# Low-rank second factors copied inside SBUF instead of through DRAM: two adapter layers in float32 parts

## The reference, cut to what matters

```
# x: (8, 128, 512), float32; one W0 of eight and one LoRA pair per batch
c0  = einsum('bsi,boi->bso', x, weight[itok_B_3_7])                 # layer 0, per-batch W0
y   = einsum('bsd,od->bso', c0, W1) + bias                          # layer 0, W1 shared
low = einsum('bsr,bor->bso', einsum('bsd,brd->bsr', c0, A0), B0)    # rank 16, adapter by segment
x1  = x + y + where(use_lora, low, 0)
c1  = x1 @ W2.T + b2 + scale * (x1 @ a1.T) @ b1.T                   # layer 1, rank 16 per batch
out = x1 + (c1 @ W3.T + b3) + routed experts of rank 32 on c1       # needs a max over all tokens
```

## Time and profile before

| | |
|---|---|
| Median of 3 runs | 135.06 us (134.25 to 137.37) |
| The profiled execution, its own time | 134.48 us |
| Its span, first to last instruction | 132.5 us |
| PE busy / weight loads | 120.9 us (91%) / 103.3 us (78%) |
| DVE / ACT / POOL busy | 83.6 us (63%) / 56.5 us (43%) / 22.5 us (17%) |
| Mean granted TensorE clock | 0.974 |
| DMA | 23.04 MB, 174 GB/s over the span |

### The profile page before, as it was taken

How to read it: one execution, slowest core, us unless ns; L and a number is a source line. 1 busy time by engine, 2 the same in 40 slices (tenths; PEclk the granted TensorE clock), 3 DMA queues, 4 the chain that set the end, 5 groups by cost and what they waited for, 6 DMA issues and landing times.

```text
span 132.5 us, 1890 instructions
## 1 busy us (share of the span) xinstructions
PE 120.9 (91%) x703; PEld 103.3 (78%) x703; DVE 83.6 (63%) x172; ACT 56.5 (43%) x94; POOL 22.5 (17%) x30
## 2 busy tenths in 40 slices
PE   6999999999829999999818999999989999999992
PEld 2488777888719999998717898999978878688891
DVE  0599299848967496754299376087995557431671
ACT  3374499459977374905914613153051011031000
POOL 3077815040047505000041000000000000000000
PEclk9999999999995999999997799999999999999999
DMA  3999965999389993896980000000000000000673
GB/s 108 383 393 413 404 251 140 332 398 327 95 357 380 294 329 101 287 376 203 409 326 4 0 0 0 5 0 0 0 0 0 5 0 0 0 0 0 227 272 137
DMA packets 7752, 23.04 MB, mean 174 GB/s; under 512 B 800, under 2 KB 1184, under 8 KB 7488
## 3 DMA queue, kind: packets, MB, share of 16 engines
q1 hardware_dynamic: 4784, 13.06, 26.7%
q0 software_dynamic: 2624, 9.44, 20.3%
q10 hardware_dynamic: 336, 0.44, 0.9%
HBM read 18.64 MB, written 4.29 MB: 173 GB/s over the span
## 4 chain that ended last, share of the span: by engine, by line
PE 59%; DMA 15%; DVE 15%; issue 4%; ACT 3%; SPq 1%; ACTq 0%; DVEq 0%
PE bank L851 45%; DMA b_rows<-c_lo 7%; DVE w_lo L542 5%; DMA x_in<-in_x 5%; DMA b<-b_rows 4%; PE bank L963 3%; PE bank L953 3%; DVE c_row L747 2%; PE bank L956 2%; PE bank L959 2%; DVE m_lo L581 2%; PE bank L888 1%; DVE bm_parts L740 1%; DVE x_lo L533 1%; ACT w_hi L381 1%
## 5 line engine op out<-in xcount | busy, mean ns | idle before, releaser
L336 POOL DMA_INDIRECT w_in<-in_W,rows_i x16 | 16.8, 1048 | 30.4 <-DVE w_lo L542 12.5
L851 PE MATMUL bank<-c_hi,w_hi 128*128 128x256 f32 x64 | 18.8, 294 | 2.9 <-DMA b<-b_rows 2.9
L542 DVE TENSOR_TENSOR w_lo<-w_in,w_hi 128x1024 fp32r<-128x1024 f32 x16 | 19.1, 1220 | 2.8 <-ACT w_hi L381 2.7
L851 PE MATMUL bank<-c_lo,w_hi 128*128 128x256 f32 x64 | 18.8, 294 | 0.0
L851 PE MATMUL bank<-c_hi,w_lo 128*128 128x256 f32 x64 | 18.8, 294 | 0.0
L381 ACT CAST w_hi<-w_in 128x1024 fp32r<-128x1024 f32 x16 | 16.1, 1047 | 3.5 <-DMA w_in<-in_W,rows_i 3.5
L851 PE MATMUL bank<-w_hi,x_hi 128*128 128x512 f32 x32 | 13.7, 428 | 3.1 <-issue 2.9
L851 PEld LDWEIGHTS bank<-c_hi,w_hi 128*128 128x128 f32 x64 | 12.8, 200 | 3.2 <-issue 3.0
L851 PE MATMUL bank<-m_hi,x_hi 128*128 128x512 f32 (+1 forms) x36 | 13.8, 385 | 0.0
L851 PE MATMUL bank<-m_hi,x_lo 128*128 128x512 f32 (+1 forms) x36 | 13.2, 367 | 0.0
L851 PE MATMUL bank<-w_hi,x_lo 128*128 128x512 f32 x32 | 13.2, 413 | 0.0
(11 more groups left out here) (181 smaller groups left out, 241.9 us busy)
## 6 DMA issues: line engine op xcount, KB each, us to landing
w_in<-in_W SPq DMA_DIRECT2D x5, 512.0 KB, 4.9
x_in<-in_x SPq DMA_DIRECT2D x4, 512.0 KB, 7.3
out_dram<-w_in SPq DMA_DIRECT2D x7, 256.0 KB, 3.0
be<-be_rows SPq DMA_DIRECT2D x1, 1120.0 KB, 5.1
b<-b_rows SPq DMA_DIRECT2D x1, 1024.0 KB, 4.7
w_in<-in_W SPq DMA_DIRECT2D x1, 1024.0 KB, 9.1
be_rows<-low_t SPq DMA_DIRECT2D x1, 840.0 KB, 5.2
b_rows<-c_lo SPq DMA_DIRECT2D x1, 768.0 KB, 4.6
```

The costliest lines, as they stand in the source:

```text
L336: nc.gpsimd.indirect_dma_start(w_in[:, slot, half * h:half * (h + 1)], None, W0, row).then_inc(w_landed[b][h], 16)
L542: nc.vector.tensor_tensor(part(w_lo[:, b % 2], h), raw(b, h), f32(part(w_hi[:, b % 2], h)), ALU.subtract).then_inc(w_lo_done, 1)
L851: ins = mm(o, st, mv, start=start and n == 0, stop=stop and n == len(parts) - 1)
```

## The change

1. The trip through DRAM is gone. `spread` now issues, for each pair i and each of the 4 groups g, one SBUF to SBUF copy of 32 rows: 16 transfers of 64 KB for `b0` and 16 of 70 KB for `be`, all on SP. The rows of the adapter tables are ordered by batch, so that a pair's 32 rows lie together, and the transposes of the first factors lose their reordering view (`by_pair`).
2. SP's list: W1 waits for the first half of W0 of batch 1 instead of for g0. Then b0 of pairs 0 and 1, x of pair 2 (no longer behind W0 of batch 3), b0 of pairs 2 and 3, x of pair 3, and the 16 copies of `be`.
3. PE waits for `b0_landed[i]` of its pair only; `low1_high(0)` on ACT waits for all 16 copies of `be` instead of the stores; DVE waits for all copies of `b0` before `c0_low(2)`.
4. Order of the lists: the split of `b0` goes ahead of `w_high(1)`/`w_low(1)`; the last split of `be` goes from behind `x1_high(0, 1)` to ahead of `w_high(3)`/`w_low(3)`; the split of `bm` goes from the tail into the loop's last round, ahead of `x1_high(2, 1)`/`x1_low(2, 1)`.

```diff
@@ SP
-            sp.wait_ge(g0_landed, 16)
             sp.wait_ge(w2_lo_done, 4)
             sp.wait_ge(w3_lo_done, 4)
+            sp.wait_ge(w_landed[1][0], 16)
             ...
-            def spread(parts, rows, stored):
-                src = f32(parts[:, 0]).unsqueeze(1).to_broadcast([P, G - 1, parts.shape[-1]])
-                sp.dma_start(rows[0:G - 1].rearrange("g p d -> p g d"), src).then_inc(stored, 16)
-                sp.dma_start(rows[G - 1], f32(parts[:, 1])).then_inc(stored, 16)
-            def gathered(rows):
-                return rows.rearrange("g (k i) d -> (g k) (i d)", i=NP)
+            def spread(t, parts, i, landed):
+                for g in range(G):
+                    sp.dma_start(f32(t[K2 * g:K2 * (g + 1), i]),
+                                 f32(parts[K2 * i:K2 * (i + 1), 0 if g < G - 1 else 1])).then_inc(landed, 16)
             sp.wait_ge(b0_hi_done, 1)
             sp.wait_ge(b0_done, 1)
-            spread(b0_parts, b0_rows, b0_stored)
-            sp.wait_ge(b0_stored, 32)
-            sp.dma_start(f32(flat(b0[:])), gathered(b0_rows)).then_inc(b0_landed, 16)
+            spread(b0, b0_parts, 0, b0_landed[0])
+            spread(b0, b0_parts, 1, b0_landed[1])
             sp.wait_ge(a0_ready, 1)
-            sp.wait_ge(w_landed[3][1], 16)
             load_x(2)
+            spread(b0, b0_parts, 2, b0_landed[2])
+            spread(b0, b0_parts, 3, b0_landed[3])
+            sp.wait_ge(a1_ready, 1)
+            load_x(3)
             ...
-            spread(be_parts, be_rows, be_stored)
-            sp.wait_ge(a1_ready, 1)
-            load_x(3)
-            sp.wait_ge(be_stored, 32)
-            sp.dma_start(f32(flat(be[:])), gathered(be_rows)).then_inc(be_landed, 16)
+            for i in range(NP):
+                spread(be, be_parts, i, be_landed)
@@ low1_high
-                    act.wait_ge(be_stored, 32)
+                    act.wait_ge(be_landed, 16 * NP * G)
@@ ACT
             nc.scalar.copy(flat(b1_hi), bank[7][:]).then_inc(b1_hi_done, 1)
+            act.wait_ge(g0_landed, 16)
+            nc.scalar.copy(b0_parts[:, 0], rows0[:, D:2 * D]).then_inc(b0_hi_done, 1)
             ...
             w_high(1)
-            act.wait_ge(g0_landed, 16)
-            nc.scalar.copy(b0_parts[:, 0], rows0[:, D:2 * D]).then_inc(b0_hi_done, 1)
@@ ACT (DVE's list changes in the same places, with the lo parts)
             low0_high(0)
+            act.wait_ge(bes_summed, 1)
+            nc.scalar.copy(be_parts[:, 0, D:], bes_f[:]).then_inc(bes_hi_done, 1)
             w_high(3)
             ...
+                if i == NP - 1:
+                    act.wait_ge(late_landed, 16)
+                    nc.scalar.copy(bm_parts[:], bm4).then_inc(bm_hi_done, 1)
                 x1_high(i - 1, 1)
@@ DVE
             x_low(2)
+            for i in range(NP):
+                dve.wait_ge(b0_landed[i], 16 * G)
             c0_low(2)
@@ layer_b
-                    pe.wait_ge(b0_landed, 16)
+                if h == 0:
+                    pe.wait_ge(b0_landed[i], 16 * G)
```

More of the change, by code:

```diff
@@ L52, in place, with build @@
         at += w
-def build(nc, x, W0, W1, W23, g0, g1, scale, early, al, late, b0_rows, be_rows, out):
+def build(nc, x, W0, W1, W23, g0, g1, scale, early, al, late, out):
     ctx = ExitStack()
@@ L167, in build @@
         g0_landed, g1_landed, s_landed = sem("g0_landed"), sem("g1_landed"), sem("s_landed")
-        b0_stored, be_stored, w3_landed = sem("b0_stored"), sem("be_stored"), sem("w3_landed")
-        b0_landed, be_landed = sem("b0_landed"), sem("be_landed")
+        w3_landed = sem("w3_landed")
+        b0_landed, be_landed = [sem(f"b0_landed{i}") for i in range(NP)], sem("be_landed")
         late_landed = sem("late_landed")
@@ L490, in _ @@
             nc.scalar.copy(ae[:, :, 0:NS], ae_f[:]).then_inc(ae_hi_done, 1)
-            act.wait_ge(bes_summed, 1)
-            nc.scalar.copy(be_parts[:, 0, D:], bes_f[:]).then_inc(bes_hi_done, 1)
             for i in range(2, NP):
@@ L504, in _ @@
                 c0_high(2 * i + 1)
+                if i == NP - 1:
+                    act.wait_ge(late_landed, 16)
+                    nc.scalar.copy(bm_parts[:], bm4).then_inc(bm_hi_done, 1)
                 x1_high(i - 1, 1)
-            act.wait_ge(late_landed, 16)
-            nc.scalar.copy(bm_parts[:], bm4).then_inc(bm_hi_done, 1)
             low0_high(NP - 1)
@@ L614, in bits @@
                                                  ALU.logical_shift_right, ALU.bitwise_and))
-                bits(1, 0, NP - 1)
-                bits(2, 2, RANK - 1)
-                bits(3, 6, 1)
+                bits(1, 5, NP - 1)
+                bits(2, 0, RANK - 1)
+                bits(3, 4, 1)
                 bits(4, 4, 1)
@@ L670, in _ @@
             nc.vector.tensor_tensor(flat(b1_lo), bank[7][:], f32(flat(b1_hi)), ALU.subtract).then_inc(b1_lo_done, 1)
-            w_low(1)
             dve.wait_ge(b0_hi_done, 1)
@@ L674, in _ @@
                                     ALU.subtract).then_inc(b0_done, 1)
+            w_low(1)
             dve.wait_ge(aet_ready, 1)
@@ L701, in _ @@
             low0_low(0)
+            dve.wait_ge(bes_hi_done, 1)
+            nc.vector.tensor_tensor(be_parts[:, 1, D:], bes_f[:], f32(be_parts[:, 0, D:]),
+                                    ALU.subtract).then_inc(bes_done, 1)
             w_low(3)
@@ L714, in _ @@
             nc.vector.tensor_tensor(ae[:, :, NS:2 * NS], ae_f[:], f32(ae[:, :, 0:NS]), ALU.subtract).then_inc(ae_done, 1)
-            dve.wait_ge(bes_hi_done, 1)
-            nc.vector.tensor_tensor(be_parts[:, 1, D:], bes_f[:], f32(be_parts[:, 0, D:]),
-                                    ALU.subtract).then_inc(bes_done, 1)
             for i in range(2, NP):
@@ L730, in _ @@
                 c0_low(2 * i + 1)
+                if i == NP - 1:
+                    dve.wait_ge(bm_hi_done, 1)
+                    for a in (1, 3):
+                        at = slice(R * a, R * (a + 1))
+                        nc.vector.tensor_tensor(bm_parts[at], bm4[at], f32(bm_parts[at]),
+                                                ALU.subtract).then_inc(bm_done, 1)
                 x1_low(i - 1, 1)
@@ L736, in _ @@
             low1_low(NP - 2)
[L737 to L740, removed]
             dve.wait_ge(w3_landed, 16)
@@ L939, in layer_low1, with turn_rows @@
                 low_rank(bank[7][:, 0:2 * S], a1, i, x_hi[:, i], x_lo[:, i]).then_inc(low1_ready, 1)
-            def turn_rows(o, rows, by_pair):
+            def turn_rows(o, rows):
                 for c in range(C):
                     to = chunk(o[:], c)
-                    last = nc.tensor.transpose(to.rearrange("p (i k) -> p k i", k=K2) if by_pair else to, chunk(rows, c),
+                    last = nc.tensor.transpose(to, chunk(rows, c),
                                                ident[:])
@@ L981, in _ @@
             pe.wait_ge(ident_done, 1)
-            turn_rows(bank[7], rows1[:, D:2 * D], False).then_inc(b1_ready, 1)
+            turn_rows(bank[7], rows1[:, D:2 * D]).then_inc(b1_ready, 1)
             layer_a(0)
@@ L997, in _ @@
             pe.wait_ge(g0_landed, 16)
-            turn_rows(bank[6], rows0[:, 0:D], True).then_inc(a0_ready, 1)
+            turn_rows(bank[6], rows0[:, 0:D]).then_inc(a0_ready, 1)
             layer_a(1)
@@ L1011, in _ @@
                             [(small_parts[:, c], b2_parts[:, c]) for c in range(C)]).then_inc(smalls_ready, 1)
-                    turn_rows(bank[5], rows1[:, 0:D], True).then_inc(a1_ready, 1)
+                    turn_rows(bank[5], rows1[:, 0:D]).then_inc(a1_ready, 1)
                 layer_low0(i - 1)
@@ L1056, in _ @@
             pe.wait_ge(ae_done, 1)
-            pe.wait_ge(be_landed, 16)
+            pe.wait_ge(be_landed, 16 * NP * G)
             pe.wait_ge(c0_saved, NB)
@@ L1161 @@
     g0 = np.concatenate([np.zeros((RANK, 2 * D), np.float32), table(v["L0_ffn_lora_A"], v["L0_ffn_lora_B"])])
-    by_rank = np.broadcast_to(v["itok_B_1_7"].reshape(NP, 2).T[:, None, :], (2, RANK, NP))
+    by_rank = np.repeat(v["itok_B_1_7"], RANK)
     ids = np.concatenate([np.broadcast_to(v["itok_B_3_7"], (P, NB)), by_rank.reshape(P, 1),
@@ L1182 @@
         args.append(nc.dram_tensor("in_" + name, a.shape, mybir.dt.from_np(a.dtype), kind="ExternalInput").ap())
-    args.append(nc.dram_tensor("b0_rows", (G, K1, D), F32, kind="Internal").ap())
-    args.append(nc.dram_tensor("be_rows", (G, K1, D + NS), F32, kind="Internal").ap())
     args.append(nc.dram_tensor("out_dram", (NB, S, D), F32, kind="ExternalOutput").ap())
```

## The result

The changed kernel takes 128.9 us (median of 4 runs, 128.15 to 129.42) against 136.04 us before (4 runs, 134.25 to 137.37): a ratio of 0.957, 95% interval 0.946 to 0.967. It is faster by 4.3%, where 125.2 us had been forecast. The profiled execution took 129.24 us (span 126.9) against 134.48 (132.5): 5.2 us less, not 9.1.

What follows compares the result with a forecast made beforehand. PE, busy 91%, was taken to lose time in two big stops and the slow clock behind each. Removing them, less 1.0 us in the middle, plus 0.1 for bm, gave 9.1 us: 125.4, stated as 125.2, range 123.3 to 129.3 (about 85%).

Steps and rivals of the forecast that it cites:

- both stops: Before layer_b(0, 0) (`b`) and layer_a(6) (late `be`): gains 3.4 and 3.5 us, plus 1.5 and 1.6 of slow clock.
- bm account: `bm` split leaves DVE's tail: new 0.6 us stop at low1(2), one of 0.6 removed; gain 0.0 to 0.1.
- the sum: 3.4 + 1.5 + 3.5 + 1.6 - 1.0 + 0.1 = 9.1 us off the profiled 134.48, hence 125.4.
- The start: layer_b(0, 0) starts at 36.6 in place of 40.02 us: gain 3.4, bounds 2.9 to 5.1.
- the term of 1.0 us for the middle: Short new PE stops, 0.5 us at turn_c0(3), 0.3 at low0_low(1) and their like: 1.0 given back, bounds 0 to 3.
- the bad end: `be` up to 4 us late at 0.7 us per copy; ACT stops 52 to 56, giving back perhaps 3 us.
- Rival (c): W0 of batch 4 lands 2 us later; PE stops 2 to 3 us at turn_c0(3) or layer_a(4): 127 to 129, 14%.
- (b): `be` partly late, 0.6 to 0.8 us per copy; 2 to 4 us stop before layer_a(6) remains: 128 to 131, 12%.
- The third mis-sized step: Before layer_b(0, 0): early W1 brings W0 of batch 2 some 2 us earlier, W1's lo part 0.6 us earlier.
- layer_a(6) near 61.5: Sign of being right: layer_a(6), behind the second big stop at 69.92 us before, starts near 61.5 us.
- 134.25 - 10.7: Whole kernel, if all stops go and the middle gives nothing back: 123.5 us.
- The rule that spoke against it: Many small transfers should be one; some 2 us each, sixteen copies in a row 35 us if they did not overlap.

Runs made afterwards that it cites:

- the edit alone: The kernel with `be` as two held-back DRAM writes and `b0` by 16 copies, with the split of bm back in the tail: 124.91 us, ratio 0.927.
- fast version: Changed kernel, but `be` goes through DRAM, its 2 writes held until both halves of W0 of batch 4 landed; `b0` keeps 16 copies: 124.87 us, ratio 0.929.
- second profiled execution of the changed kernel: The changed kernel run again with no edit, beside three other kernels: 129.55 us, ratio 0.962, span 126.4.
- fourth experiment: Kernel before, still through DRAM, with the rest of the change (early W1, early x of pairs 2 and 3, splits moved): 130.44 us, ratio 0.984.
- quiet stretch: 68 to 82 us of the fast version, where one run added unused transfers inside SBUF with nothing else in flight: 124.15 us, span 122.2.

## Why the prediction missed

**What held.** The reading of both stops was right, and so was their removal in kind: no wait for `b`, x_high(3) without a wait, the clock at full from 20 to 90 us in both profiled executions (1.5 us given back twice: from layer_b(0, 0), 2.0 us early, to turn_c0(2), 3.4 us early, and from layer_a(6), 4.1 us early, to the end, 5.6 us early). W1 was issued at 16.98 as worked out. The bm account (one stop of 0.6 in, one out) was shown by the edit alone. The fast version's profiled execution has a span of 123.3 us and 125.0 us of time, against 125.4 of the sum, but that is in part luck: its start is 0.9 us later than forecast (37.53), and it gives nothing back in the middle, where 1.0 had been forecast.

**Where the 3.5 us are.** The sum made the span 132.5 - 9.1 = 123.4 us; it was 126.9. Three terms account for it. The start brought 1.97 us, not 3.4: 1.4 short. The middle gave back 2.24 + 0.59 = 2.8 us, not 1.0: 1.8 short. The last 0.2 lie behind layer_a(6). (The time outside the span grew by another 0.3 us, from 2.0 to 2.3.) In the second profiled execution of the changed kernel the start was as forecast (36.71, 3.3 us) and the middle gave back 1.53 + 2.15 = 3.7.

**The step that failed** is the term of 1.0 us for the middle, with `be` in time at no cost, and it rests on the price of a copy: "16 copies at SP's 0.39 us end their issue at 44.6 ... I let them land by 48". The 0.39 us came from a write to DRAM, the nearest row. A copy inside SBUF holds SP's queue for 0.62 us alone and 0.68 us in place; `be` was ready for its first copy at 39.78 (1.5 us later than worked out), the last copy was issued by 50.6, and ScalarE had them at 57.44, 6.8 us after that, where 3.4 had been allowed. So `be` was 9.4 us late: 1.5 by its start, 4.5 by the issues, 3.4 by the landing. That cost PE 0.59 us in one execution and 2.15 in the other. The prediction had named 0.7 us as the bad end ("a landing of `be` after 52 us"), and gave that case only 12%. The rows offered nothing inside SBUF, so the range of this price should have had the same weight at both ends, and 16 of them in series on one path multiply it.

**The other part of that term** is the gather of W0 of batch 4. Rival (c) had the right place and too small a chance: the gather took 7.9 and 7.2 us instead of 6.1, the stop at turn_c0(3) was 2.24 and 1.53 us instead of 0.5. By what `be` had in flight beside it, the gather took:

| `be` beside the gather | us, one execution each |
|---|---|
| 16 copies inside SBUF | 7.9, 7.2, 7.3, 6.2 |
| trip through DRAM, hi written three times | 8.2 |
| two writes to DRAM | 6.8 |
| nothing, held back until it had landed | 5.5, 5.2, 6.3, 5.9, 5.6, 5.3 |
| nothing, old order, x of pair 2 just ahead | 6.5 |

Holding `be` back removed the stop, for the copies (2.24 and 1.53 to nothing) as for the two writes (1.1 to nothing). So it is contention with `be` in flight, and the trip's 8.2 us speak against a special price of the copies: `be` goes out 14 us earlier than before, by either route. The rows overlap (6.2 with the 16 copies, 6.3 and 6.5 without), so the size of it is not settled by these single executions; the 8.2 is one execution too. That the early `be` does both things was not in the prediction: it had (b) and (c) as separate cases, and they came together.

**The third mis-sized step** is the start: "W0 of batch 2 comes 2 us earlier or so" when W1 is out of the way. Its halves came 0.1 and 0.9 us later in the profiled execution, and W1's lo part, issued 3.2 us earlier, ended 0.9 later; the 1.97 us gained lie below the bound of 2.9 "with no gain from W1". In the other profiles of this kind the first half was cast between 25.7 and 27.7. Across the profiles with the early W1 and the 16 copies of `b0` the start lies between 36.3 and 38.1. The copies beside that gather may be the cause; no run shows it, and with only 4 of them the start was 36.84, inside that spread.

**Two slips in the arithmetic.** "layer_a(6) near 61.5" leaves out the 1.0 us which the sum gives back in the middle: it should be 62.5, and 65.79 is 1.4 (start) and 1.8 (middle) behind that. PE's own work between layer_b(0, 0) and layer_a(6) was right: 24.9 us net of stops, as before (69.92 - 40.02 - 0.6 - 2.9 - 1.5). And the lower bound "134.25 - 10.7" does not follow from the terms, which give 10.1 without the middle, so 124.2.

**The rule that spoke against it.** The Trainium skill ("DMA: Bandwidth & Descriptors", Rules for kernel authors) wants many small transfers made one. As advice it was right: two writes in the place of sixteen copies, held back until the gather had landed, took 4.6 us off the kernel (129.55 against 124.91 us in one group, the latter also with the bm split in the tail, which is worth nothing). The writes alone, not held back, gave 126.73 us in another group, some 2 to 3 us less than the changed kernel's 128.9 and 129.55. The Trainium skill ("SBUF - State Buffer", The DMA setup-cost knee) gives some 2 us to each transfer; this agrees with the 2.0 us landing in quiet. As 2 us in series it did not come: the copies overlapped, one issued every 0.62 us.

**What paid.** The order of the lists and of SyncE's queue:

| medians, us | old order | new order |
|---|---|---|
| trip through DRAM | 135.3 to 136.0 | 130.4 |
| copies inside SBUF | 138.0 | 128.9 and 129.6 |

The route by itself costs 2.6 us in the old order. In the new one it saves 0.9 to 1.5 us of the medians, between groups and within the spread of the fourth experiment (128.2 to 131.6), so that is not shown; the interval of that experiment's own ratio reaches 1.002. What the copies of `b0` do is seen in the profiles: no stop for `b`, where the trip leaves 1.8 us and a slow stretch. They need not be 16: with 4 for pair 0 and DRAM for the rest the time is the same (124.95 and 124.87). Those of `be` are better as two writes, and better still held back.

## What to carry to other kernels

A route that replaces two large transfers by sixteen small ones is priced by the issue of one, times sixteen, on the path of whoever waits for the last: take that price from a row of the same kind of transfer, or treat it as unknown by a factor of two. Copy piecewise only what is consumed piecewise. When a transfer is moved ahead, look which gather it now runs beside: holding two cheap writes back until that gather had landed was worth 1.9 us between two otherwise equal kernels (medians 126.73 and 124.87, ranges 125.5 to 127.4 and 124.6 to 125.4). And change route and order one at a time: here the order paid, while the change was named after the route.

## What the runs showed of the hardware

- SyncE's queue was held 0.56 to 0.71 us (means) by a DMA from SBUF to SBUF, whether it had 32 rows of 2 KB, 128 of 512 B or 128 of 2 KB, in the quiet stretch; a write of 128 rows to DRAM held it 0.37 to 0.49 us, in the kernel before and in the fast version.
- A 64 KB copy inside SBUF landed 2.0 us after its issue with nothing beside it and 5.1 us (median) beside the gathers; eight issued in a row overlapped.
- The same gather of 512 KB took 5.2 to 6.5 us with no transfer of `be` beside it and 6.2 to 8.2 us with one, by either route.
- The length of a stop did not alone decide on the clock. Stops of 2.24 and 2.15 us were not followed by the lower level in the two profiled executions of the changed kernel. A stop of 1.80 us with the trip through DRAM was (granted clock 0.66 over 40 to 45 us), as were those of 2.69 us in two of the experiments, and of 2.87 and 2.92 before.
